# Expert phase of a cross-attention and mixture-of-experts layer: transpositions two units ahead, hidden activations two and outputs three units behind, with third buffers

## What is computed

```python
x = x + xattn(layernorm(x), ctx, ctx, mask, Wq, Wk, Wv, Wo, 16)
xt = layernorm(x).reshape(-1, 256)
scores = sigmoid(xt @ gate_w.T)
_, idx = top_k(scores + gate_b, 4)
w = take(scores, idx); w = w / sum(w) * 2.5
comb = zeros(T, 16).at[tokens, idx].add(w)
for e in range(16):
    y += comb[:, e] * ((silu(xt @ w1[e].T) * (xt @ w3[e].T)) @ w2[e].T)
y += (silu(xt @ w1_s.T) * (xt @ w3_s.T)) @ w2_s.T        # shared expert
return x + y
```

## Time and profile before

| | |
|---|---|
| median of 3 runs | 2254.79 us |
| lowest, highest | 2245.89, 2255.83 us |
| profiled execution, whole | 2257.12 us |
| its span (first to last instruction) | 2255.2 us |
| TensorE matmul busy | 2096.2 us, 93% |
| VectorE busy | 1879.3 us, 83% |
| ScalarE busy | 1680.7 us, 75% |
| GpSimd busy | 1410.9 us, 63% |

### The profile page before, as it was taken

How to read it: one execution, slowest core, us unless ns; L and a number is a source line. 1 busy time by engine, 2 the same in 40 slices (tenths; PEclk the granted TensorE clock), 3 DMA queues, 4 the chain that set the end, 5 groups by cost and what they waited for, 6 DMA issues and landing times. The chain is left out here.

```text
span 2255.2 us, 58109 instructions
## 1 busy us (share of the span) xinstructions
PE 2096.2 (93%) x16576; PEld 2020.2 (90%) x16576; DVE 1879.3 (83%) x6129; ACT 1680.7 (75%) x4795; POOL 1410.9 (63%) x2107
## 2 busy tenths in 40 slices
PE   6999999999999999999999999998898998888885
PEld 5999999999999998999999999997788897888884
DVE  6999999999999999999999999998753446666677
ACT  5988889888888888889888888988554554444431
POOL 3565655555555555878888877885655545555556
PEclk9999999999999999999999999999999999999998
DMA  6777777777777767866666656666766667788797
GB/s 190 186 176 187 191 178 187 183 183 190 174 193 177 183 173 180 218 175 176 171 179 181 174 158 166 176 167 184 248 237 226 237 234 266 261 273 276 248 309 238
DMA packets 261295, 457.32 MB, mean 203 GB/s; under 512 B 36544, under 2 KB 148672, under 8 KB 260992
## 3 DMA queue, kind: packets, MB, share of 16 engines
q1 hardware_dynamic: 235376, 383.07, 61.0%
q0 software_dynamic: 25616, 70.55, 9.8%
HBM read 141.00 MB, written 144.70 MB: 127 GB/s over the span
## 5 line engine op out<-in xcount | busy, mean ns | idle before, releaser
L773 POOL TENSOR_SCALAR E<-E,rinv 128x256 f32<-128x256 f32 x1024 | 481.1, 481 | 458.3 <-DVE rinv L1084 454.0
L959 ACT ACTIVATE E<-E,negmax 128x256 f32<-128x256 f32 x1024 | 508.7, 502 | 4.9 <-DVE negmax L1109 4.7
L1109 DVE CUSTOM_DVE_ANT_0 E<-pS,m_in 128x256 f32<-128x256 f32 x1024 | 387.1, 415 | 35.6 <-PE pS L870 32.4
L1128 DVE TENSOR_TENSOR PT_lo<-pT,PT_hi 128x512 fp32r<-128x512 f32 x512 | 350.5, 684 | 27.5 <-ACT PT_hi L977 23.3
L1529 POOL DMA_INDIRECT block<-expert_rows,slot x256 | 245.3, 958 | 185.6 <-PE epG L87 95.2
L977 ACT ACTIVATE PT_hi<-pT 128x512 fp32r<-128x512 f32 x512 | 304.8, 595 | 9.3 <-PE pT L880 0.3
L880 PE MATMUL pT<-ident,E 128*128 128x128 f32 x2048 | 306.6, 272 | 0.5 <-POOL E L773 0.5
L893 PE MATMUL pV<-PT_hi,V 128*128 128x256 f32 x1024 | 287.4, 303 | 6.4 <-DVE PT_lo L1128 6.4
L869 PE MATMUL pS<-qk_st 128*128 128x256 f32 x1024 | 268.6, 284 | 8.6 <-DMA qk_st<-qk_sp 8.4
L945 ACT ACTIVATE qk_sp<-pj 128x256 fp32r<-128x256 f32 x512 | 196.8, 385 | 104.2 <-PE pj L87 89.1
L870 PE MATMUL pS<-qk_st,qk_sp 128*128 128x256 f32 x1024 | 266.2, 282 | 0.0
(11 more groups left out here) (218 smaller groups left out, 7139.3 us busy)
## 6 DMA issues: line engine op xcount, KB each, us to landing
qk_st<-qk_sp SPq DMA_DIRECT2D x512, 192.0 KB
qk_st<-qk_sp SPq DMA_DIRECT2D x512, 128.0 KB
sorted_rows<-qk_st SPq DMA_DIRECT2D x152, 256.0 KB, 3.6
xg<-sorted_rows SPq DMA_DIRECT2D x76, 512.0 KB
expert_rows<-block SPq DMA_DIRECT2D x76, 512.0 KB
acc<-x_plus_attention SPq DMA_DIRECT2D x35, 256.0 KB
x_in<-in_x SPq DMA_DIRECT2D x32, 256.0 KB
c_in<-in_ctxT SPq DMA_DIRECT2D x32, 256.0 KB, 4.1
```

The costliest lines, as they stand in the source:

```text
L773: last = pool.tensor_scalar(e[:, t, :], e[:, t, :], rinv[:, r, t:t + 1], 1.0, ALU.mult, ALU.mult)
L959: last = act.activation(E[r][:, t, :], E[r][:, t, :], ACT.Exp, bias=negmax[:, r, t:t + 1], scale=-1.0, accum_out=rowsum[:, r, t:t + 1])
L1109: last = dve.tensor_tensor_reduce(out=E[r][:, t, :], in0=pS[g % 2][:, t, :], in1=m_in.tile(b)[:, t, :], scale=-1.0, scalar=BIG, op0=ALU.ad ...
L1128: dve.tensor_tensor(lo[:, :, :], pT[n % 2][:, :, :], f32(hi[:, :, :]), ALU.subtract).then_inc(s_ptlo, 1)
```

## The change

The pipeline over units gets deeper by one step ahead and one behind. TensorE's step becomes `transposed(i + 2)`, `gate_up(i)`, `hidden_T(i - 2)`, `down(i - 3)`; ScalarE's `evict(i - 4)`, `x_hi(i + 2)`, `gate_silu(i)`, `hidden_hi(i - 2)`; VectorE and SyncE follow. For this `exT` and `gate_act` get a third buffer each, in the free parts of the value weights' tensors that also hold two pairs of raw weights at the start. So these two places are not used again for weights 10 and 11: weights 10 to 15 go to `block0` to `block5`, each when the weight eight before it is split. PSUM stays as it is, `epT` a pair and `epH` single. GpSimd's steps, `gather_at` and `scatter_at` are not changed.

```diff
+        self.x_third = [nc.alloc_sbuf_tensor_at(f"x_third{n}", [P, D // P, S], F32R, offset=wv_at + 4 * ((2 * n + 1) * ATTENTION_WIDTH + 512))
+                        for n in range(2)]
+        self.gate_third = nc.alloc_sbuf_tensor_at("gate_third", [P, S // P, EXPERT_WIDTH], F32, offset=wv_at + 4 * (512 + D))
...
-        first, second = self.raw[e % len(self.raw)]
+        first, second = self.raw[e if e < len(self.raw) else e - len(self.raw) + len(self.wv)]
...
-            uses.append((i + 1, i + 4, PARK, b))
+            uses.append((i + 2, i + 5, PARK, b))
...
-    STEPS = range(-5, max(stores_at) + 1)
+    STEPS = range(-6, max(stores_at) + 1)
...
-        xT = [pair_of(f"exT{n}", [P, NK, S]) for n in range(2)]
-        gate_act = [sb(f"gate_act{n}", [P, NT, INTER]) for n in range(2)]
+        xT = [pair_of(f"exT{n}", [P, NK, S]) for n in range(2)] + [shared.x_third]
+        gate_act = [sb(f"gate_act{n}", [P, NT, INTER]) for n in range(2)] + [shared.gate_third]
+        NXT, NGA = len(xT), len(gate_act)
...
+        AGAIN = HELD - len(shared.wv)
...
-                sp.wait_ge(s_w13lo, e - HELD + 1)
-                sp.wait_ge(s_w2lo, e - HELD + 1)
+                sp.wait_ge(s_w13lo, e - AGAIN + 1)
+                sp.wait_ge(s_w2lo, e - AGAIN + 1)
...
             for i in STEPS:
-                if works(i + 1):
-                    transposed(i + 1)
+                if works(i + 2):
+                    transposed(i + 2)
                 if works(i):
                     gate_up(i)
-                if works(i - 1):
-                    hidden_T(i - 1)
                 if works(i - 2):
-                    down(i - 2)
+                    hidden_T(i - 2)
+                if works(i - 3):
+                    down(i - 3)
...
-                if w >= 2:
-                    act.wait_ge(s_GU, w - 1)
-                act.activation(xT[w % 2][0][:, :, :], pT[w % 2][:, :, :], ACT.Copy).then_inc(s_xhi, 1)
+                if w >= NXT:
+                    act.wait_ge(s_GU, w - NXT + 1)
+                elif w == NXT - 1:
+                    act.wait_ge(s_w13lo, 1)
+                act.activation(xT[w % NXT][0][:, :, :], pT[w % 2][:, :, :], ACT.Copy).then_inc(s_xhi, 1)
```

More of the change, by code:

```diff
@@ L1228, in expert_phase @@
             uses.append((first + 1, last + COMBINE + 2, SUM, b))
-            uses.append((i + 1, i + 4, AFTER, b))
+            uses.append((i + 2, i + 5, AFTER, b))
         else:
-            uses.append((min(i + 1, first + 1), max(i + 4, last + COMBINE + 2), SUM, b))
+            uses.append((min(i + 2, first + 1), max(i + 5, last + COMBINE + 2), SUM, b))
     uses.sort()
@@ L1447, in _ @@
             for i in STEPS:
-                if is_a("dense", i + 4) and not is_last(i + 4) and i + 4:
-                    load_dense(units[i + 4][1])
+                if is_a("dense", i + 5) and not is_last(i + 5) and i + 5:
+                    load_dense(units[i + 5][1])
                 if i == -2:
@@ L1454, in _ @@
                 for e in weights_at.get(i, ()):
-                    if e + HELD < N_EXP:
-                        load_weights(e + HELD)
+                    if HELD <= e + AGAIN < N_EXP:
+                        load_weights(e + AGAIN)
                 if i == PLACE_AT + 8:
                     spread_experts(LATE_GROUP)
[L1459 to L1462, removed]
+                if is_a("sorted", i + 6) and sorted_number(i + 6) % 2 == 0:
+                    load_sorted(i + 6)
+                if is_a("sorted", i - 4) and sorted_number(i - 4) % 2:
+                    store_sorted(i - 4)
                 for use in stores_at.get(i, ()):
@@ L1585, in gate_up @@
                         for k in range(NK):
-                            last = split_products(pe, pG[w % 2][:, t, :], [a[:, k, t * P:(t + 1) * P] for a in xT[w % 2]],
+                            last = split_products(pe, pG[w % 2][:, t, :], [a[:, k, t * P:(t + 1) * P] for a in xT[w % NXT]],
                                                   [w13s[:, k, 0:H1] for w13s in sw13], k == 0, k == NK - 1)
@@ L1618, in hidden_T @@
                 for t in range(NT):
-                    last = pe.transpose(pH[:, t * P:(t + 1) * P], gate_act[w % 2][:, t, :], shared.ident[:, :])
+                    last = pe.transpose(pH[:, t * P:(t + 1) * P], gate_act[w % NGA][:, t, :], shared.ident[:, :])
                 last.then_inc(s_hT, 1)
@@ L1777, in combine @@
                 dve.wait_ge(s_cg[n % NCB], TOPK * DMA * (n // NCB + 1))
-                if joins[b] and at_dense[b] + 3 <= gather_of[n] + COMBINE:
+                if joins[b] and at_dense[b] + 4 <= gather_of[n] + COMBINE:
                     dve.wait_ge(s_yde, turn_of[b] + 1)
@@ L1790, in _ @@
             for i in STEPS:
-                if is_a("dense", i - 3):
-                    b = units[i - 3][1]
+                if is_a("dense", i - 4):
+                    b = units[i - 4][1]
                     if joins[b]:
```

38 lines of the change are left out of this document (21 added, 17 removed).

## The result

| | before | changed |
|---|---|---|
| median | 2250.54 us (7 runs, 2245.89 to 2255.83) | 2237.57 us (7 runs, 2235.09 to 2240.31) |
| ratio to before | | 0.9942, 95% interval 0.9926 to 0.9958 |
| profiled execution | 2257.12 us | 2235.09 us, span 2233.2 |

The change is faster by 0.6%, 13 us, where 40 were forecast; 2237.57 lies outside the forecast's range of 2195 to 2236.

What follows compares the result with a forecast made beforehand. It took TensorE to be held by signals arriving late while GpSimd issues indirect DMAs, mostly at exT_lo. Terms -26 - 16 - 7 + 2.5 + 8 = -38.5, rounded to -40, took 2254.8 to 2215 us, range 2195 to 2236.

Steps and rivals of the forecast that it cites:

- (2): Hidden transposition: holds, when TensorE's signals arrive late, each get 0.95 us cheaper, 27 times: -26 us.
- (3): Short TensorE waits before gate-and-up matmuls, at most 1.3 us each, 17.8 us in all: -16 us.
- the second stretch: TensorE from unit 75 to 158: a sign of being right was 300 us falling to about 275.
- rival B: Holds grow with TensorE's lead because GpSimd issues more: 2240 to 2260 us; chance 0.20.
- (4): TensorE's clock: a third of the 20 us lost at the lower clock level goes, -7 us.
- (5): Start of the expert phase: first weight splits up to 2.6 us later, +2.5 us, between 0 and 5.
- (6): GpSimd in the gathers: faster TensorE shrinks its pauses and lengthens rows of DMAs, +8 us, bounds 0 and 22.
- Rival A: All TensorE bubbles go, as a third buffer would end them: 2156 to 2190 us; chance 0.14.
- C: Two units' signals released at once lengthen GpSimd's rows and the holds: slower, about 2290 us; chance 0.07.
- D: VectorE and DMA take over as limit in the third stretch, win about half: 2235 us; chance 0.12.

Runs made afterwards that it cites:

- e4: The change with every indexed gather replaced by a plain DMA of 128 rows in order, leaving out the selection of rows; 2169.63 us, ratio 0.9635.
- e1: The kernel before with only the earlier transpositions (third exT, unit i + 2), hidden part, down and outputs unmoved; 2236.0 us, ratio 0.9933.
- e2: The kernel before with only the later hidden transposition, down and output (third gate_act); 2261.44 us, ratio 1.0045.
- e16: The change with two epH and down and output one more unit later, with late signals; 2258.58 us, ratio 0.9993.
- e9: The change with two epH and down and output one more unit later, in a set without late signals; ratio 0.9959.
- set 5: Runs with late signals of the kernel before (2259.72 us) and the change with two epH and down and output one unit later (ratio 0.9993).
- e3: The change with a second epH from unit 17 on; 2237.17 us, ratio 0.9935.
- e12: The kernel before, unchanged, run again in a set without late signals; ratio 1.0007.

## Why the prediction was off

**What bounds the kernel**: right. TensorE's idle time in the expert phase goes with GpSimd's indirect DMAs (e4: 31.6 us to 0.3), and exT_lo was the wait that held TensorE (e1 has the whole effect, e2 none). That it is a state of the set of runs and not of the kernel was in no view of one trace.

**(2) Long holds, -26, and (3) short waits, -16**: these are the terms that failed. exT_lo's 51.7 us went and ehT_lo's rose from 6.1 to 23.9, within the 20 to 50 that the prediction named; but the idle time fell by 17.3 us, not 42, and the second stretch took 283.9 us where about 275 was named. The waits that (2) prices, exT_lo and all at the hidden transposition, went from 51.7 + 8.9 = 60.6 to 48.7 us, by 12. The short ones of (3) went from 17.8 to 10.8, by 7, where 16 were taken, and the stops inside a group took 3 back.

Part of it lies in the sum itself. It took 0.95 us off each of 27 holds, from one place where TensorE lost 2.95 us, while the mean of those waits was 1.9. And it called the slack at epH 1.7 us, only 0.35 more than the 1.35 that exT_lo had had. In the 27 + 28 places in which TensorE had waited before the matmuls, 0.35 us each is 19 us (an estimate from the prediction's own slacks), and 12 + 7 is what went: this fits holds that nearly all reach TensorE again, 56 times in place of 55, at the next buffer.

The other part is that the sum took each hold as fixed from outside, 4.2 us of lateness, and counted only how much further TensorE could work in it. By that, e16, with some 2 us more for the hidden half, had to win clearly more than the change. It has 43.9 us idle from 1841 to 2141, as before has (44.1), and the ratio 0.9993; ScalarE's standstills are longer, and TensorE stops without a wait, for 2.4, 5.7 and 21.1 us in before, change and e16. That is one set, in which the change did not run, so how much of the shortfall of the change is due to holds that grow stays open. The median, 2237.57, lies between the forecast's range and that of rival B (2240 to 2260). B's mechanism, a GpSimd that issues more because TensorE is further, shows in part: rows of four or five gathers went from 15 before to 24 in the change, and e16 has rows of six. But the stops inside a group are no part of B.

**(4) The clock, -7**: right in kind and too small. By the granted clock of the windows the time at 1.2 GHz fell from 19 + 18 + 3 = 40 us to 4.5 + 5.7 + 7.1 = 17, worth about 11.5 us. This term alone came out larger than forecast. The granted clock is printed to hundredths, and half a hundredth is up to 6 of 600 us at the lower level, so 3 us of time, in either kernel. The Trainium skill, TensorE: Matmul & The Clock Gate, has in its section on HAM oscillation that waits between groups of matmuls let the clock fall. The first two windows agree, 0.96 and 0.97 before and 0.99 after, with the longest wait 2.4 us in place of 4.8; the third does not, for its clock fell from 0.98 to 0.96 while its longest wait fell from 2.2 to 1.0 us. Idle time and clock together make 28.8 us, more than the 23.6 won from unit 6 to 183; 5.2 us of busy time came back, for which I have no row; the rounding of the clock alone could make it.

**(5) The start, +2.5**: the first weight split moved from 1577.14 to 1579.54 as worked out, but unit 6's matmuls began at 1605.51 against 1606.45. It cost nothing in these two executions.

**(6) GpSimd's pace, +8**: in the middle it can't be read apart from the idle time of (2) and (3); the end was missed. The last group's 64 gathers take from their first start to the last end 95.6 us in both kernels, so what TensorE gains behind unit 158 is worth nothing. And the outputs' stores come a step later while the gathers' plan is kept: the first gather of that group waits 7.71 us, before 5.60:

```profile
2153.24 0.98 POOL L1529 DMA_INDIRECT block<-expert_rows,slot  x1 [5.60 <-PE epG L87]
...
2247.82 1.06 POOL L1529 DMA_INDIRECT block<-expert_rows,slot  x1 [0.30 <-issue]
```

```profile
2130.13 0.94 POOL L1534 DMA_INDIRECT block<-expert_rows,slot  x1 [7.71 <-DMA expert_rows<-block]
...
2224.59 1.16 POOL L1534 DMA_INDIRECT block<-expert_rows,slot  x1 [0.30 <-issue]
```

From unit 158's matmuls to that first gather it is 12.5 us before and 15.9 in the change. The part from unit 183's matmuls to the end grew from 27.3 to 29.9 us.

The sum by what the profiled executions show: start -0.9, idle -17.3, clock -11.5, other busy time +5.2, end +2.6, and 0.1 of rounding: -22, where the prediction had -38.5. From -22 between the profiled executions to -13 between the medians it is the 6.6 and 2.5 us by which these two executions stood above and below theirs. Rival A is out: TensorE stayed idle for 64.5 us. The Trainium skill (Perfetto Trace Analysis, Optimization Strategy) says that a repeated bubble can mean too few buffers. e9, without late signals and with no idle time in 193 us, agrees with it; e16, the same kernel with 43.9 us idle in 300, does not, so there the measurement decides. Rivals C and D are out too. In the change no row of gathers from 1841 to 2130 is longer than five, and VectorE is busy 191.68 of 283.90 us. The stretch from unit 158 to 183, where D looked, won nothing, but VectorE and the DMAs are not what holds it: between ScalarE's activations of these two units lie 88.2 us before, 88.0 in the change and 71.6 in e4.

**What stays open**: what delays the signals in some sets and not in others on the same chip. Whether the stops inside a group have the same cause: they could also be TensorE waiting for its own instructions, which no run here tested. Whether the change too would gain nothing in set 5, or the deeper kernel as much as the change in the sets where that gained. What a third ehT that is used would do. And whether a looser pace of GpSimd helps or hurts with late signals. Among the kernels that keep the selection of rows none had a ratio to before that is better than the change's beyond the intervals.

## What to carry to other kernels

A buffer more moves a stall to the next buffer of the chain: before pricing it, set the slack there beside the slack here (1.7 and 1.35 us in this case), for only the difference is won at each stall. A stall that a slow message causes need not be of fixed length either: ask what each engine does in the extra time, and where it can be had, price the cover from a kernel that has it (here e16), beside the change in one set of runs. Two waits on the same event stand one behind the other: follow the semaphore, not the buffer, to see whether a second buffer frees anything (e3). Where a stage is moved later, look for whatever is planned by step numbers behind it (here the gathers of the last group). Compare medians: of the 22 us between the two profiled executions 9 were scatter. And read an experiment's edit again when it surprises: a buffer that is allocated is not yet one that is used (the third ehT of e16).

## What the runs showed of the hardware

- The same kernel took 2251 to 2260 us in some sets of runs and 2152 to 2154 in others, two of them on the same chip. The difference lies in the expert phase: unit 0's matmuls begin between 1577 and 1585 us in all of them, and units 75 to 158 of the kernel before take 300 us in the one case (before) and 243 in the other (e12).
- In the sets with late signals other engines read TensorE's results late while GpSimd issues indirect DMAs one after another: by 4.2 us in before, by 2.7 us in the change (epH at 1934.97). DMAs without indices at the same places take GpSimd 547 ns in place of 957 and leave TensorE 0.3 us idle in 229 (e4). In the sets without, the indirect DMAs take 970 ns, up to 182 in a row, and ScalarE never waits for TensorE over 0.6 us (e9).
- In the sets with late signals TensorE also stopped between two matmuls of one group that have no wait, for up to 1.7 us at a time: 2.4 us in all before, 5.7 in the change, 21.1 in e16 (another set).
